# Four edits to a graph-and-FFN network kernel: edge counting by ramps between the first products, gate columns in a class product, router products between others, last tile in halves

## The reference

```python
x = x + gat0(ln(x))    # 8 heads + 1, over edges and self-loops
x = x + ffn0(ln(x))    # tokens 0-5: routed "class" tokens; the others: a plain FFN
x = x + gat1(ln(x))
x = x + ffn1(ln(x))
x = x + gcn2(ln(x))
x = x + ffn2(ln(x))    # 8 experts, one per token
x = x + rgcn3(ln(x))   # 34 relations, then a GCN
x = x + ffn3(ln(x))    # 8 experts, two per token
```

## Time and profile before

| | |
|---|---|
| median of 3 runs (lowest, highest) | 1392.44 us (1392.18, 1395.44) |
| the profiled execution | 1392.8 us |
| its span, first to last instruction | 1391.0 us |
| granted clock of TensorE, mean | 0.981 of 2.4 GHz |
| busy, share of the span: PE, PEld, DVE, ACT, POOL | 94%, 83%, 72%, 45%, 16% |
| HBM traffic, mean | 163 GB/s |

### The profile page before, as it was taken

How to read it: one execution, slowest core, us unless ns; L and a number is a source line. 1 busy time by engine, 2 the same in 40 slices (tenths; PEclk the granted TensorE clock), 3 DMA queues, 4 the chain that set the end, 5 groups by cost and what they waited for, 6 DMA issues and landing times.

```text
span 1391.0 us, 21373 instructions
## 1 busy us (share of the span) xinstructions
...
## 2 busy tenths in 40 slices
...
GB/s 346 152 189 213 167 167 208 191 144 93 99 202 199 166 170 216 180 121 118 121 103 159 212 166 151 161 195 171 151 156 195 176 151 152 191 177 128 184 72 23
DMA packets 103718, 227.32 MB, mean 163 GB/s; under 512 B 16688, under 2 KB 34672, under 8 KB 103684
## 3 DMA queue, kind: packets, MB, share of 16 engines
...
HBM read 216.56 MB, written 10.29 MB: 163 GB/s over the span
## 4 chain that ended last, share of the span: by engine, by line
PE 81%; DVE 12%; ACT 2%; DMA 2%; issue 2%; DVEq 0%; ACTq 0%; SPq 0%
PE bank L418 80%; DVE w_lo L1181 3%; DVE stats L1219 1%; ACT w_hi L892 1%; DMA w_in<-L_gnn_W 1%; PE bank L457 1%; DVE h_lo L1181 1%; DVE spare L1394 1%; DVE a_bc L1394 1%; DVE x_sb L1181 1%; PE bank L514 1%; DMA w_in<-L_gnn_W_root 1%; DVE xT_lo L1181 1%; DVE neg_b L1184 0%; DMA x_sb<-x 0%
## 5 line engine op out<-in xcount | busy, mean ns | idle before, releaser
L1181 DVE TENSOR_TENSOR w_lo<-w_in,w_hi 128x2304 fp32r<-128x2304 f32 (+4 forms) x162 | 396.5, 2477 | 61.0 <-ACT w_hi L892 60.7
L892 ACT ACTIVATE w_hi<-w_in 128x2304 fp32r<-128x2304 f32 (+4 forms) x162 | 328.1, 2062 | 224.4 <-PE bank L418 197.2
L418 PE MATMUL bank<-w_hi,xT_hi 128*128 128x384 f32 (+3 forms) x942 | 324.7, 345 | 6.9 <-DVE xT_lo L1181 4.5
L418 PE MATMUL bank<-w_lo,xT_hi 128*128 128x384 f32 (+3 forms) x942 | 310.1, 341 | 0.0
L418 PE MATMUL bank<-w_hi,hid_hi 128*128 128x512 f32 (+2 forms) x858 | 293.9, 342 | 5.8 <-DVE hid_lo L1181 3.5
L418 PE MATMUL bank<-w_lo,hid_hi 128*128 128x512 f32 (+2 forms) x858 | 271.6, 337 | 0.0
L418 PE MATMUL bank<-w_hi,xT_lo 128*128 128x384 f32 (+3 forms) x942 | 248.0, 342 | 0.0
L418 PE MATMUL bank<-w_hi,hid_lo 128*128 128x512 f32 (+2 forms) x858 | 224.6, 339 | 0.0
L418 PEld LDWEIGHTS bank<-w_hi,xT_hi 128*128 128x128 f32 (+1 forms) x942 | 179.1, 190 | 36.3 <-issue 8.2
L418 PEld LDWEIGHTS bank<-w_hi,hid_hi 128*128 128x128 f32 (+1 forms) x858 | 161.8, 189 | 42.3 <-issue 5.3
L418 PEld LDWEIGHTS bank<-w_lo,xT_hi 128*128 128x128 f32 (+1 forms) x942 | 179.2, 190 | 13.6
...
## 6 DMA issues: line engine op xcount, KB each, us to landing
...
```

Source lines behind the costliest of these rows:

```text
L418: return pe.matmul(out, lhsT, rhs, start=start, stop=stop, **kw)
L892: act.activation(out, ps, func, **kw).then_inc(mark, 1)
L1181: return dve.tensor_tensor(out, a, b, op)
```

## The change

**Counting (layer 0).** The one-hot source row of an edge becomes a ramp, max(0, n + 1 - src), and the counts come out of two first differences along the row (`ramp_sum`, `ramp_step`). VectorE makes the destinations, the types and one ramp of a batch's four; ScalarE makes the other three with `Relu` and a bias (batch 0 is VectorE's alone). TensorE runs batch 0 ahead of the first product, then k-steps of the first head with a batch behind each from k = 3 of tile 0 on (nine batches), then the last six. `all_dst` moves from `a_bc` to `neg_b`, so head 0's vectors are loaded early, and VectorE takes head 0's dots and h_lo of tile 0 between batches. The second copy of the counts is made in the scores of head 0. The bias of layer 0 is added to x at the end of the GAT. SP clears `table` only when the first weights have landed. ScalarE loads `key_row` after the batches.

**ffn0.** The 12 gate vectors are loaded at the start, turned by TensorE at the end of GAT 0, and stand as 12 more columns of the class product. Their squares are taken there too. The low part of ffn0's second weights and the load of the tanh tables come ahead of the gate steps. The atoms are turned ahead of the plain product. 8 idle products follow the gates where 19 did.

**Routers.** In ffn2 and ffn3 the router's products stand between the k-steps: three ahead of each step of tile 0, six ahead of each of the first three steps of tile 1.

**ffn3.** Biases, gelu, weighting and transposes go tile by tile. The output product waits for one buffer pair at a time. Tile 1's output product is made in two halves of 384 columns, in banks 6 and 7, whose moments and scaling read PSUM, and each half is stored by itself.

The diff, cut to its core:

```diff
+                    for p in range(2):
+                        sp.wait_ge(w_full[p], 16)
                     sp.dma_start(table.rearrange("(p t) n -> p t n", p=P),
                                  zrow[:, :].unsqueeze(1).to_broadcast([P, ROWS // P, N])).then_inc(cleared, 16)
...
                 if layer == 0:
                     pe.wait_ge(e_mask, 1)
+                    pe.wait_ge(e_kept, 2)
                 seed((0, 1, 2))
-                spread(9 * layer)
...
+                if layer == 0:
+                    pe.wait_ge(ld_gate, 16)
+                    for k in range(K):
+                        pe.transpose(bank[4][:, k * 2 * NCLS:(k + 1) * 2 * NCLS], gp[:, k * P:(k + 1) * P], ident[0:2 * NCLS, 0:2 * NCLS])
+                    pe.wait_ge(gp_diag, 1)
+                    mm(bank[4][0:NCLS, K * 2 * NCLS:(K + 1) * 2 * NCLS], ones[0:2 * NCLS, 0:NCLS], gdiag[:, :]).then_inc(gp_turned, 1)
+                idle(3, 18 if layer == 0 else 20)
...
+            def count(step_of):
...
+                count_batch(0)
+                b = 1
+                for m, banks in ((0, (5, 6)), (1, (3, 4))):
+                    for k in range(K):
+                        last = step_of(m, banks, k)
+                        if k == K - 1:
+                            last.then_inc(*((h_mm, 1) if m == 0 else (w_used, 2)))
+                        if m or k > 2:
+                            count_batch(b)
+                            b += 1
+                for b in range(b, ET // G):
+                    count_batch(b)
...
-                last = mm3([(bank[3][0:NCLS, 0:ATOMS * FH], of_w(1)(k, FH, (ATOMS + 1) * FH))],
+                last = mm3([(bank[3][0:NCLS, 0:CLASS_COLS], of_w(1)(k, FH, FH + CLASS_COLS))],
...
+            pe.wait_ge(atoms_kept, 1)
+            for a in range(ATOMS):
+                last = pe.transpose(bank[6][0:FH, a * NCLS:(a + 1) * NCLS], atoms[:, a * FH:(a + 1) * FH], ident[0:NCLS, 0:NCLS])
+            last.then_inc(atoms_t, 1)
...
             last.then_inc(w_used, 1)
-            pe.wait_ge(atoms_kept, 1)
-            for a in range(ATOMS):
-                last = pe.transpose(bank[2][0:FH, a * NCLS:(a + 1) * NCLS], atoms[:, a * FH:(a + 1) * FH], ident[0:NCLS, 0:NCLS])
-            last.then_inc(atoms_t, 1)
...
-            idle(0, 19)
+            idle(0, 8)
...
+            def with_router(s, m, ready):
+
+                def route_step(k):
+                    return mm3([(bank[0][:, m * 8:(m + 1) * 8], part(rw_hi, rw_lo, slice(0, P), slice(k * 8, (k + 1) * 8)))],
+                               part(xT_hi, xT_lo, slice(0, P), k, slice(m * P, (m + 1) * P)), k == 0, k == K - 1)
+
+                def both(k):
+                    ready(k)
+                    if m == 0:
+                        route_step(k)
+                    elif k < 3:
+                        route_step(2 * k)
+                        last = route_step(2 * k + 1)
+                        if k == 2:
+                            last.then_inc(f_mm[s], 1)
+                return both
...
+            idle(4, 8)
+            for m in range(M):
+                pe.wait_ge(f_dve[3], 4 + m)
+                for j in range(4):
+                    for e in (2 * j, 2 * j + 1):
+                        last = pe.transpose(bank[HT3_BANKS[j]][0:HID3 + 1, (e % 2) * N + m * P:(e % 2) * N + (m + 1) * P],
                                             ge[:, m, e, :], ident[:, :])
-                last.then_inc(f_mm[3], 1)
-            pe.wait_ge(f_dve[3], 7)
+                    if m == 1:
+                        last.then_inc(f_mm[3], 1)
...
+            nodes(0, NODE_BANKS, hidden(0), w_out, hidden_low).then_inc(w_used, 1)
+            for j, mark in enumerate((f_mm[3], w_used)):
+                nodes(0, [[(6 + j, 0, HALF, j * HALF)]], hidden(1), w_out).then_inc(mark, 1)
...
+            act.wait_ge(consts, NCONST)
+            act.wait_ge(e_src, 1)
+            for b in range(1, ET // G):
+                act.wait_ge(e_used, b + 1)
+                for g in range(ACT_RAMPS):
+                    last = act.activation(all_src[:, b % RING, g, 0:N], iota[:, :], ACT.Relu, bias=edge_f[:, 0, b * G + g:b * G + g + 1])
+                last.then_inc(e_ramp, 1)
+                if b == 5:
+                    act.wait_ge(h_mm, 1)
+                    keep_tile(0, h_sb, h_kept)
+                    keep_tile(0, h_hi, h_high)
+                if b == 11:
+                    act.wait_ge(w_used, used(0))
+                    keep_tile(1, h_sb, h_kept)
+            keep_tile(1, h_hi, h_high)
+            act.wait_ge(e_cnt, 1)
+            keep(ramp_sum[:, 1, :], bank[1][:, 0:N], e_kept)
...
-            act.wait_ge(h_low, 2 * (HEADS + 1))
-            act.dma_start(gp[:, :, :], t["L0_ffn_gate_pair"]).then_inc(ld_gate, 16)
...
             act.wait_ge(e_deg, 1)
             keep(sd[:, :], deg[:, :], e_std, ACT.Sqrt)
             act.wait_ge(f_dve[0], 1)
             keep(gate[:, 8:11], gate[:, 0:3], f_act[0], ACT.Sqrt)
+            act.activation(gate[:, 36:38], bb[:, :], ACT.Tanh)
+            act.wait_ge(f_mm[0], 1)
+            keep(atoms[:, :], bank[3][0:NCLS, 0:CLASS_COLS], atoms_kept)
             act.wait_ge(f_dve[0], 2)
             keep(gate[:, 24:25], gate[:, 22:23], f_act[0], ACT.Tanh, scale=0.5)
...
+            def hot(b, ramps):
+                a = b % RING
                 dve.wait_ge(e_used, b + 1)
                 tt(all_src[:, a, :, N:N + REL], iota[:, 0:REL].unsqueeze(1).to_broadcast([P, G, REL]),
-                   edge_f[:, 2, bass.ds(b * G, G)].unsqueeze(2).to_broadcast([P, G, REL]), ALU.is_equal)
+                   edge_f[:, 2, b * G:(b + 1) * G].unsqueeze(2).to_broadcast([P, G, REL]), ALU.is_equal)
                 for g in range(G):
-                    for j, out in ((0, all_src[:, :, :, 0:N]), (1, all_dst)):
-                        last = dve.tensor_scalar(out[:, a, g, :], iota[:, :], edge_f[:, j, bass.ds(b * G + g, 1)], None, ALU.is_equal)
+                    last = dve.tensor_scalar(all_dst[:, a, g, :], iota[:, :], edge_f[:, 1, b * G + g:b * G + g + 1], None, ALU.is_equal)
+                for g in ramps:
+                    last = ts(all_src[:, a, g, 0:N], iota[:, :], edge_f[:, 0, b * G + g:b * G + g + 1], add_, 0.0, mx)
                 last.then_inc(e_hot, 1)
 
-            with dve.Fori(0, ET // G // RING) as i:
-                for a in range(RING):
-                    one_hot(i * RING + a, a)
-            for a in range(ET // G % RING):
...
+            hot(0, range(G))
+            low(1, 0)
+            first_out = scores_b[:, :, :, :].rearrange("p a m n -> p (a m n)")[:, 0:D]
+            for b in range(1, ET // G):
+                hot(b, range(ACT_RAMPS, G))
+                if b == 7:
+                    tile_dots(0, 0, first_out)
+                    tile_low(0, 0)
+            tile_dots(0, 1, first_out)
...
-            step(last)
+            dve.tensor_copy(ramp_sum[:, 0, :], bank[0][:, 0:N])
...
+            dve.wait_ge(e_kept, 1)
+            dve.tensor_copy(ramp_step[:, :, 1:2], ramp_sum[:, :, 0:1])
+            step(tt(ramp_step[:, :, 2:N + 1], ramp_sum[:, :, 1:N], ramp_sum[:, :, 0:N - 1], ALU.subtract))
...
-            dve.tensor_reduce(deg[:, :], cnt[:, 0, :, :], AX.X, add_).then_inc(e_deg, 1)
+            step(dve.memset(hrow[FH:FH + 1, :], 1.0))
+            low_chunk(C_FFN0 + 1, parts=(1,))
...
-            for r in range(2):
-                step(dot(junk[0:NCLS, :], gp[:, r, :], gp[:, r, :], gate[:, 1 + r:2 + r]))
-                last = dot(junk[0:NCLS, :], cls, gp[:, r, :], gate[:, 3 + r:4 + r])
-                if r == 0:
-                    step(last)
-            last.then_inc(f_dve[0], 1)
...
+            dve.wait_ge(atoms_kept, 1)
+            step(own(atoms[:, ATOMS * FH:CLASS_COLS]))
+            step(dve.tensor_reduce(gate[:, 3:5], gsel[:, :, :], AX.X, add_))
...
-            last.then_inc(f_dve[3], 1)
-            dve.wait_ge(f_act[3], 2)
+                last.then_inc(f_dve[3], 1)
             for m in range(M):
+                dve.wait_ge(f_act[3], 2 + m)
                 dve.tensor_copy(ge[:, m, :, HID3], lg[:, 14, m, :])
-                last = tt(ge[:, m, :, 0:HID3], h_sb[:, m, :].rearrange("p (e h) -> p e h", e=EXP3),
-                          lg[:, 14, m, :].unsqueeze(2).to_broadcast([P, EXP3, HID3]), mul)
-            last.then_inc(f_dve[3], 1)
+                tt(ge[:, m, :, 0:HID3], h_sb[:, m, :].rearrange("p (e h) -> p e h", e=EXP3),
+                   lg[:, 14, m, :].unsqueeze(2).to_broadcast([P, EXP3, HID3]), mul).then_inc(f_dve[3], 1)
...
+            halves = [slice(j * HALF, (j + 1) * HALF) for j in range(2)]
+            for j in range(2):
+                dve.wait_ge(*((f_mm[3], 7) if j == 0 else (w_used, used(C_FFN3 + 2))))
+                last = dve.bn_stats(stats[:, 1, j, :], bank[6 + j][:, 0:HALF])
+            step(last)
+            dve.bn_aggr(mv[:, 1, :], flat(stats[:, 1, :, :])).then_inc(ln_var, 1)
+            moments_taken[0] += 1
```

(3 more changed lines are left out.)

290 lines of the change are left out of this document (167 added, 123 removed).

## The result

The changed kernel takes 1369.63 us (median of 4 runs, 1366.45 to 1376.49) against 1393.37 (4 runs): ratio 0.9841, 95% interval 0.9822 to 0.9861, so faster by 1.4 to 1.8%, a small difference but clear of the noise. In a second set of runs it took 1372.14 (4 runs, 1368.55 to 1375.11) against 1392.38 (7 runs), ratio 0.9855 (0.9831 to 0.9878). The forecast was 1373.0, range 1365 to 1382. What stands out is the spread: 10 us between executions of the changed kernel, 3 to 5 us before. A low window is a stretch in which TensorE was granted a clock well under 1.00 of full speed.

What follows compares the result with a forecast made beforehand. TensorE was taken to bound the heads and relations, with losses where it waits for VectorE and to low clock. Start 6.9, ffn0 3.2, ffn2 2.6 and ffn3 7.0 sum to 19.7 off 1392.8; forecast 1373.0, range 1365 to 1382.

Steps and rivals of the forecast that it cites:

- TensorE sets the pace of the counting: Start: VectorE and ScalarE keep up with TensorE, so the counts end at 50.2 instead of 59.16, 9.0 us earlier.
- the term for a batch: Start: each counting batch was charged 1.17 us of TensorE time, beside 1.04 us for a k-step.
- From the counts to alpha 9.4 us: Start: the chain behind the counts takes 9.4 us, so alpha comes at 59.6 and `turn` 8.4 us earlier.
- A low clock behind the longer wait, 1.5 us: Behind `turn`: a TensorE wait of some 3.2 us may bring a low clock, charged 1.5 us; start 6.9 earlier.
- ffn0 4.0 us, 3.2 with the clock: ffn0: output product 4.0 us earlier, less 0.8 for a low clock reaching into products that count: 3.2.
- The steps that I listed from the low part to `wdiag`: ffn0: two gate steps, selection of two columns and 2.5 us more, from 333.7 to `wdiag` at 336.5.
- The routers, 2.6 in ffn2 and 3.0 of ffn3's share: Routers between k-steps remove low windows behind them: ffn2 2.6 us earlier, and 3.0 us lost in ffn3's window regained.
- Between products of 512 columns I expect the clock to hold: ffn2: interleaved router products keep the full clock, recovering what is left of 3.4 us; 2.6 taken.
- rival 1: Clock takes part back: low windows behind `turn`, in ffn0 and the routers' stages, 6.5 us less gain, 1379.6; chance 0.20.
- ffn3's routing ends last: ffn3: routing ends at 1353.2 and two bias additions at 1355.3, behind tile 1's products at 1352.3; VectorE comes last.
- The low window behind the last output product stays, at no gain: ffn3: the wait ahead stays about 6 us, so the window 1366 to 1370 at 0.57 only shifts; no gain.
- The tail 3.3 us: Behind the last product: the copy gone and half the moments taken earlier, so 3.3 us instead of 4.9.

Runs made afterwards that it cites:

- d3: The kernel before the change, run once more for its low windows; no separate time given; the windows behind the router blocks lost 3.4 us in ffn2, 1.7 in ffn3.
- c7: Changed kernel with four unused dots of 768 numbers put back on VectorE ahead of ffn0's gate steps: 1377.01 us.
- c6: Changed kernel with ffn0's atoms turned behind the plain product, as before the change; gate columns stay: 1370.71 us.
- d2: Changed kernel with the low part of ffn0's second weights behind the gates on VectorE again: 1373.70 us (4 runs).
- c2: Changed kernel with the router's 36 products in one block again, in ffn2 and ffn3: 1372.02 us (median of 3 runs).
- c3: Changed kernel with the last tile's output product, moments, scaling and store in one piece: 1372.47 us.

## Why the prediction was right, and where it was off

The case was right: the kernel is faster, and both times lie in the range. Of the four parts, counting and ffn0 gain as they were meant to, by experiment, and so do the halves of the last tile. The routers aren't shown to. No run took ffn3's order by tiles back alone, so what it gives is read from before and after only. By its steps:

1. *TensorE sets the pace of the counting*: right. The counts ended at 48.0, not 50.2, as the term for a batch was mis-sized: I took 1.17 us, the busy time of one, as the distance between batches. Neighbouring groups overlap; batch and k-step together take 2.06 us, not 2.21, and batches alone 1.03 each. Eight times 0.15 and seven times 0.14 are 2.2 us. The Trainium skill, "Perfetto Trace Analysis", in its part on TensorE's start and end times, says that the end shown is estimated; these rows agree, and starts are the numbers to subtract.
2. *From the counts to alpha 9.4 us*: 9.8 measured (48.0 to 57.78). `turn` 10.2 earlier instead of 8.4.
3. *A low clock behind the longer wait, 1.5 us*: right in kind. It costs 1.2 to 2.3 us in four of nine traces with that wait, 0 to 0.4 in the others, 0.8 on the mean. The start is 9.4 us earlier so, where 6.9 were forecast: the largest miss of a term.
4. *ffn0 4.0 us, 3.2 with the clock*: right. From the end of the class product to the output product it was 15.38 before (15.91 in d3) and is 11.39 in most traces: 4.0 us. From its start it is 19.3 and 19.9 before, 15.4 to 17.0 after, since the clock often falls in the class product itself, ahead of the place where I expected it; on the mean 3.3. c7 shows that the dots carry it. The wait of about 2.7 us for `wdiag` is there only when the atoms are turned behind (2.68 in c6); I had overlooked the wait for `atoms`, which takes its place and costs nothing (c6). That the low part stood in the way behind `wdiag` is right, but it stands in the way as much ahead of the gates: moving it gave nothing, and cost 0.3 us (d2). The steps that I listed from the low part to `wdiag` add up to 3.3 us, not the 2.8 that I used; 2.5 were measured in c6.
5. *The routers, 2.6 in ffn2 and 3.0 of ffn3's share*: half right. A block of small products is followed by a low window in seven of seven traces. The step "Between products of 512 columns I expect the clock to hold" failed in four of eleven traces in ffn2 and in six of ten in ffn3, where first product to output product took 27.3 to 28.9 us instead of 24.2 (24.0 forecast; 29.4 and 27.9 before). I also read one low window in ffn2 where there were two. ffn2 is 3.2 us shorter on the mean than before, but so it is in c2, with the block: that the number came out near 2.6 is luck. Here rival 1 came true in part of the executions.
6. *ffn3's routing ends last*: right. VectorE adds the four biases behind routing without a wait, and TensorE waits 2.03 us for the weighted hidden rows.
7. *The low window behind the last output product stays, at no gain*: wrong in most executions. From the first output product to the last product it was 18.1 and 19.6 us before, with such a window, and is 16.7 in ten of twelve traces, 17.3 in after and c3. This gain of 1.5 us or more, put at nothing, makes up for part of what the clock took in the stage's first products: ffn3 from first to last product is 4.4 us shorter on the mean (1.3 to 6.7), where 5.4 were forecast.
8. *The tail 3.3 us*: 3.4. The shorter last store (0.5 us) was missing from the sum.

The terms as measured, on the mean: start 9.4, ffn0 3.3, ffn2 3.2, ffn3 4.4, tail 2.0, together 22.3, against 19.7 forecast and 20.2 and 23.7 between the medians. That the forecast came within 3.4 us owes something to chance: the start gave 2.5 more than its term, and the clock alone moves an execution by several us (the executions differ by up to 10).
